# A transformer layer on one core: opening, drain and end of the program re-ordered

## The reference

```
qk = x @ Wqk.T + bqk;  v = x @ Wv.T + bv            # 8 heads, 8 numbers each
attn = softmax(q @ k.T) / 8;  o = attn @ v
x1 = layernorm(x + o @ Wo.T + bo)
g = silu(x1 @ Wg.T);  u = x1 @ Wu.T                 # Wg, Wu: 1792 x 512, int4 with a scale per 128 columns
y = layernorm(x1 + (g * u) @ Wd.T)                  # Wd: 512 x 1792, the same
```

## Time and profile before

| | |
|---|---|
| median of 3 runs | 521.55 us (521.29 to 521.72) |
| profiled execution | 521.81 us |
| its span, first to last instruction | 519.7 us |
| mean granted TensorE clock | 0.998 |
| PE busy | 501.1 us, 96% |
| DVE busy | 413.0 us, 79% |
| ACT busy | 405.5 us, 78% |
| POOL busy | 255.7 us, 49% |

### The profile page before, as it was taken

One profiled execution on the slowest core, in us unless ns is written; L12 is line 12 of the kernel. 1 busy time (PEld: TensorE's weight loads), 2 busy tenths in 40 slices (PEclk: granted clock), 3 DMA queues, 4 the chain that ended last, 5 costly groups with the idle time before them and its releaser, 6 DMA issues.

```text
span 519.7 us, 8086 instructions
## 1 busy us (share of the span) xinstructions
PE 501.1 (96%) x2976; PEld 193.2 (37%) x2976; DVE 413.0 (79%) x705; ACT 405.5 (78%) x558; POOL 255.7 (49%) x295
## 2 busy tenths in 40 slices
PE   8899999999999999999999999999999999999994
PEld 3222222323222322234444444444444444444441
DVE  3699999989999997368878778778668666788677
ACT  1522888998899989877888888888888888888880
POOL 9100091823100715073464676664997962648741
PEclk9999999999999999999999999999999999999999
DMA  6410018576530005700031121140020020000022
GB/s 192 136 68 5 21 35 211 182 144 125 91 59 1 3 5 103 276 7 1 1 59 24 20 43 21 20 62 1 1 81 1 0 83 0 3 0 1 0 81 81
DMA packets 30151, 29.20 MB, mean 56 GB/s; under 512 B 19489, under 2 KB 21921, under 8 KB 29857
## 3 DMA queue, kind: packets, MB, share of 16 engines
q1 hardware_dynamic: 26688, 22.67, 15.7%
q0 software_dynamic: 3424, 6.03, 6.3%
HBM read 24.37 MB, written 4.23 MB: 55 GB/s over the span
## 4 chain that ended last, share of the span: by engine, by line
PE 79%; DVE 7%; POOL 5%; ACT 5%; issue 2%; DMA 1%; SPq 0%; DVEq 0%; POOLq 0%; ACTq 0%
PE ps L1123 16%; PE ps L1135 16%; PE ps L1157 16%; PE ps L1068 9%; PE ps L1039 6%; PE ps L963 6%; DVE mxh L1249 4%; ACT pbuf L760 3%; PE ps L892 3%; POOL x L617 2%; PE ps L1051 1%; PE ps L902 1%; PE ps L1016 1%; POOL stack L663 1%; DMA arena<-xT 1%
## 5 line engine op out<-in xcount | busy, mean ns | idle before, releaser
L1249 DVE TENSOR_REDUCE mxh<-ps 128x1 f32<-128x512 f32 x256 | 157.0, 680 | 6.5 <-PE ps L963 5.3
L760 ACT ACTIVATE pbuf<-ps,gamma 128x1024 f32<-128x1024 f32 x128 | 140.5, 1114 | 16.2 <-PE ps L1039 11.2
L841 ACT ACTIVATE ps<-ps,ratio 128x512 f32<-128x512 f32 x168 | 106.5, 659 | 40.4 <-PE ps L1123 37.3
L1157 PE MATMUL ps<-wd,stack 128*128 128x512 f16 x440 | 129.7, 379 | 0.7 <-POOL stack L663 0.6
L1123 PE MATMUL ps<-arena,wg 128*128 128x512 f16 x448 | 115.5, 379 | 0.1
L1135 PE MATMUL ps<-arena,wu 128*128 128x512 f16 x448 | 115.3, 379 | 0.1
L1423 DVE TENSOR_TENSOR ps<-ps,stack 128x512 f32<-128x512 f32 x128 | 87.8, 695 | 33.4 <-PE ps L1157 31.7
L847 ACT ACTIVATE ps<-ps,ratio 128x512 f32<-128x512 f32 x156 | 98.9, 659 | 6.6 <-PE ps L1135 2.3
L661 POOL CAST stack<-pbuf 128x512 f16<-128x512 f32 x55 | 33.5, 609 | 76.5 <-DVE pbuf L1398 76.5
L1423 DVE TENSOR_TENSOR ps<-ps,pbuf 128x512 f32<-128x512 f32 x76 | 52.6, 695 | 23.2 <-PE ps L1157 22.5
L1068 PE MATMUL ps<-pbuf,arena 128*32 128x256 f32 x832 | 66.5, 391 | 1.7 <-ACT avt L767 1.7
(11 more groups left out here) (120 smaller groups left out, 387.4 us busy)
## 6 DMA issues: line engine op xcount, KB each, us to landing
arena<-xT SPq DMA_DIRECT2D x16, 256.0 KB, 5.8
x<-x SPq DMA_DIRECT2D x2, 2048.0 KB, 10.0
out<-x SPq DMA_DIRECT2D x3, 1024.0 KB, 4.2
stack<-down_ratios SPq DMA_DIRECT2D x1, 2048.0 KB, 9.6
wg<-gq POOLq DMA_DIRECT2D x4, 448.0 KB, 7.3
wu<-uq POOLq DMA_DIRECT2D x4, 448.0 KB, 7.4
wd<-dq POOLq DMA_DIRECT2D x2, 896.0 KB, 10.3
pbuf<-down_ratios SPq DMA_DIRECT2D x1, 1536.0 KB, 6.2
```

The source lines that it names most:

```text
L760: nc.scalar.activation(pbuf[:, pi % 4, :].rearrange("p (a n) -> p a n", a=2), ps[:, at:at + 2, :], ACT.Exp, scale=gamma[:, n // (ALL // B) ...
L841: nc.scalar.activation(gbank[t % 2], gbank[t % 2], ACT.Copy, scale=gr[:, t % G, c:c + 1])\
L1157: mm = nc.tensor.matmul(bank[k], mparts[:, a, t % NM, k * P:(k + 1) * P], wd[:, i, :], start=(i == 0 and a == 0), stop=(a == 1), skip_grou ...
L1249: nc.vector.tensor_reduce(mxh[:, f % 2, qh, half:half + 1], ring_bank("first", n), AX.X, ALU.max)\
```

## The change

On every engine parts of the stream are re-ordered or replaced:

- Opening: the row maxima are read straight from PSUM without the bias, and the largest bias magnitude is added. Four small matmuls with a broadcast operand put the row of maxima on all 128 partitions at once, so that `cast_scales`, `place_scales` and the ring's `cast` go. The zeroing of the second batch's v goes from DVE to POOL; the first batch's is moved behind the first row maximum. The second of the first three placed row sets is copied by DVE, not ACT.
- Drain: `wo` of block 1 in steps 54 and 55, of block 2 in 57 and 58 (before: 54 and 56, 60 and 62), `avT` of unit 6 in step 59 (before 57). Gate and up of tile 0 are computed in steps 61 to 63, group by group, and group 3 between step 63 and the last `av_whole`; their scaling is all on DVE. The PE stream of the feed-forward begins at period 1. `turn_x1(0)` is issued ahead of the store of the down ratios.
- Feed-forward: the tail work of block 3 in periods 1 and 2 (before 0 and 1); `HELD` is 5, so tiles 0 and 1 go down in period 5, tiles 2 and 3 in period 6 (before: 0 and 1 in period 4, then one each). Residual scaling in periods 26, 27, 33, 34, 35 and 40 to 44.
- End: ACT subtracts the mean of tiles 0 and 1 while the inverse is made, and scales tiles 0, 1 and 3. DVE centres tile 3 and applies both to tile 2. ACT issues one of the four last stores.

```diff
-HELD = 4
+HELD = 5
-        TOPS_AT = {(2, 1): "tops", (4, 1): "cast"}
+        TOPS_AT = {(2, 1): "tops"}
-        ASIDE = {DRAIN: ("attT", 1, 0), DRAIN + 1: ("wo", 1, 0), DRAIN + 3: ("wo", 1, 1), DRAIN + 4: ("avT", LASTF, 0),
-                 DRAIN + 6: ("attT", 2, 0), DRAIN + 7: ("wo", 2, 0), DRAIN + 9: ("wo", 2, 1)}
+        ASIDE = {DRAIN: ("attT", 1, 0), DRAIN + 1: ("wo", 1, 0), DRAIN + 2: ("wo", 1, 1), DRAIN + 3: ("attT", 2, 0),
+                 DRAIN + 4: ("wo", 2, 0), DRAIN + 5: ("wo", 2, 1), DRAIN + 6: ("avT", LASTF, 0)}
-            last = {0: [[], [tail[0]], [], [tail[1]]], 1: [[], [tail[2]], [], [tail[3]]]}
+            last = {1: [[], [tail[0]], [], [tail[1]]], 2: [[], [tail[2]], [], [tail[3]]]}
+        IN_DRAIN = {(group, 0, c) for group in ("gate", "up") for c in range(C)}
+        GATES = ALL - C + 1
-        RESIDUAL_AT = 28
+        RESIDUAL_AT = (26, 27, 33, 34, 35, 40, 41, 42, 43, 44)
...
+            turn_x1(0)
             sp.wait_ge(s_draw, 5)
             sp.dma_start(spread.rearrange("g n -> (g n)").rearrange("(p m) -> p m", p=P), down_s).then_inc(s_stored, 16)
             sp.wait_ge(s_stored, 16)
-            turn_x1(0)
...
-                nc.tensor.transpose(dst[0:1, 0:P], tops[:, 2:3], ident[:]).then_inc(s_rf if b else s_turned, 1)
+                for own in range(2):
+                    for kind in range(2):
+                        at = HD * (kind != own)
+                        mm = nc.tensor.matmul(dst[own * HD:(own + 1) * HD, at:at + HD], tops[:, 2:3].to_broadcast([P, HD]),
+                                              ident[:, kind * HD:(kind + 1) * HD], start=True, stop=True)
+                mm.then_inc(s_rf if b else s_turned, 1)
...
             for n in range(DRAIN, ALL):
                 scores(n, 0)
+                if n >= GATES:
+                    if n == GATES:
+                        pe.wait_ge(s_aside, len(copied))
+                        pe.wait_ge(s_gu, 16 * 2 * C)
+                        pe.wait_ge(s_x1t[0], 16 * BT)
+                    gate(0, n - GATES)
                 for use in aside_at(n, 1):
                     turn(*use)
                 scores(n, 1)
                 for use in turns_at(n, 1):
                     turn(*use)
                 av_whole(n - 1)
+                if n >= GATES:
+                    up(0, n - GATES)
+            gate(0, C - 1)
+            up(0, C - 1)
             av_whole(ALL - 1)
...
-            for k in range(2):
-                row_maxima(0, k)
+            row_maxima(0, 0)
+            clear_first_v()
+            bias_magnitude()
+            row_maxima(0, 1)
             combine_tops(0)
             scale_row(0)
-            place_scales(0)
             low_parts()
+            keep_first_q()
...
             mean_variance(0)
             att_out(1)
-            down_ratios()
             for t in range(2):
                 add_output(1, t)
             apply(0)
+            for t in range(2, BT):
+                add_output(1, t)
+            att_out(2)
+            down_ratios()
+            for t in range(2):
+                add_output(2, t)
             scale_ratios()
             for t in range(2, BT):
-                add_output(1, t)
+                add_output(2, t)
             normalise(LASTF)
-            att_out(2)
-            for t in range(BT):
-                add_output(2, t)
...
+            for c in range(C - 1):
+                scale_gate(0, c)
+                scale_up(0, c)
...
+            dve.wait_ge(s_st, 2 * NB + 3)
+            nc.vector.tensor_scalar(x1[:, NB * BT - 1, :], bank[3], mv[:, 3, 0:1], None, ALU.subtract).then_inc(s_cent3, 1)
+            dve.wait_ge(s_rstd, 2 * NB + 1)
+            nc.vector.tensor_scalar(x1[:, NB * BT - 2, :], bank[2], mv[:, 2, 0:1], rstd[:, 2:3], ALU.subtract, ALU.mult)\
+              .then_inc(s_res, 1)
```

More of the change, by code:

```diff
@@ L705, in _ @@
                         apply(blk, p - RESULT_AT[blk] - 2)
+            for k in range(2):
+                pool.wait_ge(s_st, 2 * NB + k)
+                nc.gpsimd.tensor_scalar(negm[:, k:k + 1], mv[:, k, 0:1], -1.0, None, ALU.mult).then_inc(s_neg, 1)
             inverse(2 * NB - 1, slice(0, 2), 2 * NB + 1)
@@ L809, in _ @@
             act.wait_ge(s_fill, 3)
-            for n in range(3):
-                keep(n)
+            keep(0)
+            keep(2)
             project_v(0)
@@ L838, in scale_gate @@
             def scale_gate(t, c):
+                if ("gate", t, c) in IN_DRAIN:
+                    return
                 act.wait_ge(s_gf[t % 2], C * (t // 2) + c + 1)
@@ L881, in _, with centre, scale_result @@
                 slot(p, 3)
+            def centre(k):
+                act.wait_ge(s_neg, k + 1)
+                nc.scalar.activation(x1[:, (NB - 1) * BT + k, :], bank[k], ACT.Identity, bias=negm[:, k:k + 1])\
+                  .then_inc(s_cent, 1)
+            def scale_result(k):
+                x1_t = x1[:, (NB - 1) * BT + k, :]
+                act.wait_ge(s_rstd, 2 * NB + k // 2)
+                if k < 2:
+                    act.wait_ge(s_cent, k + 1)
+                else:
+                    act.wait_ge(s_cent3, 1)
+                nc.scalar.activation(x1_t, x1_t, ACT.Copy, scale=rstd[:, k:k + 1]).then_inc(s_resa, 1)
+            for k in range(2):
+                centre(k)
+            for k in (0, 1, 3):
+                scale_result(k)
+            act.wait_ge(s_resa, 3)
+            act.dma_start(out[NB * BT - 1], x1[:, NB * BT - 1, :]).then_inc(s_out, 16)
         @block.tensor
@@ L1033, in scores @@
                     pe.wait_ge(s_vc, 2 * B)
-                    pe.wait_ge(s_kept, len(placed))
+                    pe.wait_ge(s_kept, len(placed) - 1)
+                    pe.wait_ge(s_kept1, 1)
                 else:
@@ L1071, in av, with gate, up @@
                 mm.then_inc(s_av, 1)
+            def gate(t, c):
+                blk, i = divmod(t, G)
+                if t >= 2 or c:
+                    pe.wait_ge(s_gs[t % 2], C * (t // 2) + c)
+                for a in range(2):
+                    mm = nc.tensor.matmul(gbank[t % 2], wg[:, c, i * P:(i + 1) * P], x1v[blk][:, a, c, :, :],
+                                          start=(c == 0 and a == 0), stop=(a == 1), skip_group_check=True)
+                mm.then_inc(s_gf[t % 2], 1)
+            def up(t, c):
+                blk, i = divmod(t, G)
+                if t >= 2 or c:
+                    pe.wait_ge(s_us[t % 2], C * (t // 2) + c)
+                elif t == 1:
+                    pe.wait_ge(s_ave, NB * NG)
+                for a in range(2):
+                    mm = nc.tensor.matmul(ubank[t % 2], wu[:, c, i * P:(i + 1) * P], x1v[blk][:, a, c, :, :],
+                                          start=(c == 0 and a == 0), stop=(a == 1), skip_group_check=True)
+                mm.then_inc(s_uf[t % 2], 1)
             def piece(p):
@@ L1176, in _ @@
                 for k, (group, c) in enumerate(((gate, 0), (up, 0), (gate, 1), (up, 1))):
-                    if p < TILES:
+                    if p < TILES and (group.__name__, p, c) not in IN_DRAIN:
                         group(p, c)
-                    if 1 <= p <= TILES:
+                    if 1 <= p <= TILES and (group.__name__, p - 1, c + 2) not in IN_DRAIN:
                         group(p - 1, c + 2)
@@ L1219, in scale_row @@
                 dve.wait_ge(s_row, 5 * b + 3)
[L1220 to L1233 removed]
+                nc.vector.reciprocal(unit[:, b:b + 1], row[:, 2:3]).then_inc(s_row, 1)
+                nc.vector.tensor_tensor(gamma[:, b:b + 1], row[:, 2:3], row[:, 3:4], ALU.mult).then_inc(s_row, 1)
             def low_parts():
[L1237 removed]
+                dve.wait_ge(s_row, 4)
                 for k in range(2):
@@ L1442, in _ @@
                 slot(p, 0)
-                if p < EARLY:
+                if p < EARLY and ("up", p, 0) not in IN_DRAIN:
                     scale_up(p, 0)
-                if 1 <= p <= EARLY:
+                if 1 <= p <= EARLY and ("up", p - 1, 2) not in IN_DRAIN:
                     scale_up(p - 1, 2)
@@ L1462, in _ @@
                 slot(p, 2)
-                if p < EARLY:
+                if p < EARLY and ("up", p, 1) not in IN_DRAIN:
                     scale_up(p, 1)
```

164 lines of the change are left out of this document (77 added, 87 removed).

## The result

| | before | after |
|---|---|---|
| median | 521.54 us (521.29 to 521.72, 4 runs) | 526.48 us (526.14 to 527.69, 4 runs) |
| after / before | | 1.0099 [1.0082, 1.0117] |
| profiled execution, its span | 521.81, 519.7 us | 526.74, 524.7 us |
| mean granted TensorE clock | 0.998 | 0.994 |

The change costs 4.9 us. 520.6 was forecast, in a range of 518.4 to 522.4, so both the sign and the range were wrong.

What follows compares the result with a forecast made beforehand. PE, busy 96%, was taken as the main bound, with DVE bounding the first pass. Terms -1.15 - 0.45 + 2.1 + 0.35 - 0.85 - 0.95 = -0.95 gave 520.85, or 520.6 us against the median; range 518.4 to 522.4.

Steps and rivals of the forecast that it cites:

- Drain, the step that failed: Attention's last steps: tile 0's early matmuls and PE's waits make the last `av_whole` 2.6 us later, for 3.45 less afterwards.
- waits for two additions behind `down_ratios`, 0.6: Drain: PE's second `wo` of block 2 waits 0.6 us for DVE to empty its banks.
- 24.05 + 0.75 for 22.8: Drain, steps 54 to 63: PE's work 24.05 us plus waits of 0.15 and 0.6, where 22.8 was taken before.
- silu(2) was held as forecast: Feed-forward start: silu(2) waits for POOL's `inner_parts(0)`, ending at 233.2; gate(4, 0) comes at 234.0, a term of +2.1 us.
- Rival (a): Drain: silu(2) is not held, or idle time takes the new matmuls; 518.4 to 519.0 us, chance 0.23.
- rival (c): Drain, step 61: PE's gate(0, 0) waits for block 0's transposes landing late; slower, 522.7 us if at 210.8, chance 0.12.
- rival (b): Opening and residual: small gains fail through slow turns, a late memset and PE's wait on POOL moving; 521.7 us, chance 0.2.
- +0.35, -0.85: Feed-forward: periods 4 to 6 cost +0.35 us; the residual's new periods gain 0.85.
- Opening and step 4: First pass: PE's first unit at 20.05 instead of 21.22, -1.15 us; scale copies leaving DVE's queue at step 4, -0.45.
- The late memset that was weighed there: Opening: DVE's memset, if held by POOL, starts up to 1.8 us later, making the opening -0.35 to -0.95; not in the sum.
- Residual: Feed-forward: residual scaling moved to periods with POOL time to spare removes PE's wait near 385 us; -0.85, at worst 0.
- End: Kernel's end: DVE has one application after the inverse, to 516.3, and ACT stores tile 3 at 516.25; -0.95 us.

Runs made afterwards that it cites:

- e1: The changed kernel with DVE's down ratios back at their old place, ahead of block 1's additions: 522.55 us, 1.0028 of before.
- e4: The changed kernel with down ratios back, POOL's splits of tiles 0 and 1 ahead of block 3's additions, and the last store on SP: 519.61 us, 0.9960 of before.
- f6: The kernel before with opening, step 4, residual and the drain's new output product places with matching DVE order, tile 0 still behind the drain: 519.83 us, 0.9967.
- f1: The kernel before with only the opening and step 4 parts of the change: 519.47 us, 0.9960 of before.
- f3: The kernel before with only the residual's periods changed: 520.58 us, 0.9981 of before.
- e2: The changed kernel with only POOL's order altered, each split of tiles 0 and 1 ahead of two of block 3's additions: 524.24 us, 1.0048 of before.
- e3: The changed kernel with the fourth last store issued by SP instead of ACT: 527.33 us, 1.0103 of before.
- f2: The kernel before with only the end of the change, all four last stores on SP: 521.38 us, 0.9996 of before.
- f4: The kernel before with opening, step 4 and residual changed, and its old drain, feed-forward start and end: 518.37 us, 0.9938 of before.
- f5: The changed kernel with down ratios early, POOL's splits first and the old end: 519.96 us, 0.9969 of before.
- g2: The kernel before with 12 unused one-column activations ahead of ACT's silu(2), to make PE wait: 522.58 us, 1.0021 of before.
- g1: The kernel before with 24 unused one-column activations ahead of ACT's silu(2), to make PE wait: 524.78 us, 1.0060 of before.

## Why the prediction was wrong

**Drain, the step that failed.** The prediction had the last `av_whole` 2.6 later than the shift; it is 5.95 later. The 3.35 between them are two mis-sized terms.

- "waits for two additions behind `down_ratios`, 0.6". The place was right; it measured 2.49. The duration of `down_ratios` had been read where it stood before, 192 us, where POOL had nothing large in hand. In its new place POOL splits x1, and it took 3.95 (197.14 to 201.09) instead of 1.6. A row that warned of it was among those quoted, a DVE instruction of about the same size that took 1.15 near POOL's work instead of 0.22, and so was the lock. The Trainium skill ("SBUF — State Buffer", section "SBUF: two separate sides") lists a DVE instruction with two SBUF inputs beside a GpSimd instruction that reads SBUF as a case of the exclusive lock. The trace agrees for the two with two inputs, 1.27 and 1.18, and for the reciprocal with one, 0.53 in both places. But it also holds one-input instructions that took longer beside POOL: the `tensor_scalar` at 197.58, 0.51 instead of 0.22, and that of the earlier trace rows. So two inputs are not the whole condition here; what else it takes stays open. The lock was weighed for the memset and not for the five instructions that the change moved into POOL's way. e1 undoes the move: wait gone.
- PE's arithmetic without this wait, 24.05 + 0.75 for 22.8, gives +2.0. e4, which has no such wait, shows +3.6: 35.4 us from the start of the last ten reductions to the last `av_whole`, against 31.8. f6 gives 0.8 of it to the packing and leaves 2.8 for tile 0's matmuls, of whose 3.45 the prediction had let 2.2 vanish into PE's idle time. That idle time was there, but the packing had moved it: f6 has 1.1 of it in steps 61 to 63. In after PE has one gap left there, the 0.49 at 217.90, and its steps take 2.74.

**Drain, what came on top.** silu(2) was held as forecast: PE's wait 2.60, from the last `av_whole` to period 4 16.8 us (forecast 16.7), ended by POOL's second split. Rival (a) is refuted by that row, rival (c) by the absence of any wait at PE's gate(0, 0), and rival (b) by f1 and f3, where the small gains came in full. The slowest of them stood at 522.7, so none reached what was measured. But the price of a wait was taken as its length. The waits of 2.5 and 2.6 also bring the clock down in part of the runs, a net 1.3 us in the profile of after; the prediction's sum had no term for the clock. From period 4 to the first statistics of the end -0.5 was forecast (+0.35, -0.85) and +0.9 measured; with the 1.3 taken off it is -0.4, so the terms themselves were sound. The profiles of after and e2 show one fall and that of e3 two; e1's ten runs show it come and go. The Trainium skill says of the moment at which the clock rises that "it's run-variable" ("TensorE: Matmul & The Clock Gate", section "Part 1: The HAM clock gate (the "warmup" mystery)"). What varied here is another thing, of which that sentence does not speak: whether the clock falls at all behind the same wait, in four of e1's ten runs.

**Opening and step 4.** -1.15 and -0.45 were forecast; the trace shows -1.6 and -0.6, f1 -2.2. Two sizes were off: the four turns hold PE up for 0.28, not 0.7, and a v group takes 0.92 in a row of three, not 1.01. The late memset that was weighed there did not come: it ran at 11.10 beside POOL's memset and took 1.76.

**Residual.** -0.85 forecast, -1.1 by f3 (-0.85 by its trace), PE's wait gone.

**End.** -0.95 forecast; f2 shows nothing. The step "DVE has one after it, to 516.3" is true of DVE: in the timelines of after and f2 its last result comes 0.9 sooner after the first statistics. The error is the unsaid premise that DVE's last result ends the kernel. What ends it is 1.05 MB of stores, which start behind the first result and fill the transfer engines. In after the end as a whole is 0.7 longer than before (9.41 against 8.71). With the store back on SP it is some 0.45 shorter in e3's profile, which is not clear of what the end varies by, so ACT's issue of 2.04 is the likely cause and not a shown one.

**The sum against the traces.** The span grew by 5.0 where -0.95 was forecast, 5.95 more: the drain 3.35, the end 1.7, the clock 1.3, opening and step 4 -0.6, and +0.2 for the rest.

**The sum again, from the experiments.** Opening and residual -3.3 (f4); packing of the output products and the early start +1.6 (f5); end with ACT's store some +0.5 (e3's profile, the weakest of these); the wait on silu(2) +2.6 and that in the drain +2.4; that is +3.8 of 4.9. The other 1.1 is the clock. All four runs of after have a mean clock of 0.991 to 0.994, while no run of before, e4, f1 to f6 or g2 is under 0.995. So each run of after has at least one fall, a net 1.3 by its profile; the terms above are then some 0.2 too large together, and f5's is soft too (0.8 by its spans).

Left open: why the clock fell behind the drain's wait in the profiles of e2 and e3 (2.49, 2.48) and not in that of after (2.49). Open as well is whether ACT's long issue comes with its first DMA or with every one, since no kernel here issues two.

## What to carry to other kernels

Price a moved instruction at its new neighbours, not at its old duration: a rule found for one moved instruction has to be asked of every instruction that moves. Where TensorE may wait 2.3 us or more, the shortest wait behind which the fall was seen here, put the clock's fall into the range, and where a chain ends in a transfer, follow the transfer and not the engine that feeds it. Work that is put into an engine's idle time needs the idle time of the schedule after the change.

## What the hardware showed that was not expected

- Waits of PE of 2.3 to 2.6 us were followed by the lower clock level in the profiles of after, e1, e2, e3 and g1, for some 3.4 us (0.50 in full windows). Its net price was 1.3 in after, 1.1 in e1 and 1.7 in g1. In e1 it began 1.2 us after work had begun again, in e2 0.3 us before. It did not come after every such wait: not behind after's 2.49, in four of e1's ten runs, in three of g1's four. After waits of 1.17 (g2) and 0.6 (e4) it was not seen.
- A DVE instruction on 120 numbers per partition with two inputs in SBUF took 1.27 instead of 0.28 us beside a POOL instruction on 512. Beside one on 4 numbers, no shorter (1.04), it was not held (e1). A one-input `tensor_scalar` took 0.51 instead of 0.22 beside POOL's cast of 512.
- The only DMA issued by ACT took 2.04, 2.04 and 2.01 us to issue in after, e1 and e2, against 0.57 for one on SP.
- The four stores of 256 KB at the end moved at 361 and 369 GB/s in full windows of before, 385 in one of after. A last result that came 0.87 us sooner (f2) moved the end of the span by 0.2.
